# Attention pass, norm, pool table and last pass of a graph network: four programs put into one, by fifths of the nodes

## The chip, the cores and the metric

The kernel runs on one core of one Trainium2 chip. The metric is the device time of one execution in microseconds, less is better; the time of the kernel before is the median of three runs. All data are 32-bit floats except where bf16 is named.

## The reference, cut to what matters

3,125 nodes with 256 features and 53,125 edges (self loops included, sorted by target) go through four layers, each added to x after a layer norm and a rectifier. The change touches what lies between the sums of the third layer and the start of the fourth:

```python
h = jnp.maximum(_layernorm(x, axis=-1), 0.0)
x = x + _L2_gnn_ref(h, src, dst, ...)     # attention, sums over incoming edges
h = jnp.maximum(_layernorm(x, axis=-1), 0.0)
x = x + _L3_gnn_ref(h, edge_weight1, src, dst, ...)
# _L3_gnn_ref:
h = jax.nn.relu(feat @ W_pool.T + b_pool)
m = h[src] * weight
neigh = jax.ops.segment_max(m, dst, num_segments=n)
return feat @ W_self.T + b_self + (neigh @ W_neigh.T + b_neigh)
```

## The kernel before, in words

The nodes are held in SBUF as NB = 25 blocks of NT = 125 rows (`self.x`, `self.h`), and `self.hT` holds h turned around (features on the partitions). The edges are laid out in 128 lanes of LANE = 416 edges each; a pass over the edges walks the 416 steps, and each step gathers one row for each lane by an indirect DMA that GpSimd (POOL) issues.

Every stage is a `nc.Block()` of its own: one instruction stream for each engine, and a barrier of all engines at its end, so no engine begins the next stage before all have finished this one. From the third layer on there are four of them, run in this order by `build`:

1. `attention_pass`: 416 gathers of table rows, logits, exponentials and running sums on VectorE (DVE), states stored by SyncE (SP). Then the lane ends are joined, and 25 gathers (`neigh`, L1811) fetch the final state of each node's last edge, one for each block, five with one semaphore. As a fifth (five blocks) has landed, DVE divides it (L1994, L1996), adds it to x (L2000) and takes the statistics of the five blocks (L550).
2. `normalize("norm3")`: mean and scale of all 25 blocks at once on DVE, square root on ScalarE (ACT), then for each block the normed and rectified h on ACT (L589), two transposes on TensorE (PE, L599) and the copy to `hT` on DVE (L580).
3. `pool_table`: SP loads the three weight matrices and the bias as 125 equal rows, POOL loads the edge weights (L2040, L2043), PE turns the weights, and for each block PE makes two products (L2060), DVE adds the bias into `pool_out` (L2073), ACT rectifies in place (L2079), and SP stores the block to the table in DRAM. SP waits at the end for all stores.
4. `lane_max_pass`: 416 gathers from that table (L2123), each row weighed by ACT (L2148) and taken into a running maximum by DVE (L2234); beside it PE makes the products with W_self, two and a bias product of two rows (L2182, L2184). Then the lane ends are joined, 25 gathers (L2137) bring the maxima, and PE, ACT, DVE and SP finish block by block.

In each engine's stream the order is the order of the code; nothing reorders it. A matmul of 32-bit floats is two instructions in the trace (two passes), a transpose is one.

## Time and profile before

| | |
|---|---|
| median of 3 runs | 2831.26 us (2826.97 to 2834.37) |
| span of the profiled execution, first to last instruction | 2548.0 us |
| own time of the profiled execution | not listed; if it is the median, 283.3 us lie outside the span |
| PE, DVE, ACT, POOL busy in the span | 44%, 56%, 18%, 57% |
| mean granted TensorE clock | 0.698 of 2.4 GHz |

The span is what the trace can explain. The time outside it has no instruction and is taken as it is. Busy shares are averages over stages that have different limits; which engine another one waits for is read from the timeline. Where several instructions stand in one row (x25), its time is the stretch from the first's start to the last's end. PEld is the loading of the stationary matrix.

### The profile page before, as it was taken

What the parts mean: (1) busy time and instruction counts of PE and PEld (TensorE: products, weight loads), DVE (VectorE), ACT (ScalarE), POOL (GpSimd) and SP (SyncE); (2) the same over time, 40 slices, a digit from 0 to 9 for tenths busy, and PEclk for the clock granted to TensorE, in tenths of its full rate; (3) what the DMA queues carried; (4) which work ended last, traced back from release to release, by engine and by line L of the source; (5) the groups of instructions that cost most, each with busy time, mean ns of one, the idle gap of its engine ahead of it and who ended that gap; (6) DMA issues with size and microseconds to landing.
All of it is one profiled execution on the core that took longest, in us unless ns stands there. A gap on an engine that the chain in (4) does not pass through costs nothing. (4 is left out here: it accounts for less than half of the span.)

```text
span 2548.0 us, 19840 instructions
## 1 busy us (share of the span) xinstructions
PE 1127.1 (44%) x4862; PEld 811.0 (32%) x4862; DVE 1431.4 (56%) x3661; ACT 446.7 (18%) x920; POOL 1441.2 (57%) x1472
## 2 busy tenths in 40 slices
PE   5677787777657259999910000000016111111105
PEld 4566776676334135556600000000004000010004
DVE  4377777777999832222246777666754334434432
ACT  3112212221011111111200000000003333333331
POOL 3477777776246030100167777777641777777774
PEclk9799989999766559999955555555557555555557
DMA  4677777775887720000046666666622666666663
GB/s 134 193 233 232 234 232 236 232 232 173 279 266 250 236 61 5 13 10 9 15 125 210 209 208 209 210 210 208 205 66 85 212 210 207 212 212 208 208 212 126
DMA packets 210401, 447.75 MB, mean 176 GB/s; under 512 B 46661, under 2 KB 119226, under 8 KB 210287
## 3 DMA queue, kind: packets, MB, share of 16 engines
q1 hardware_dynamic: 140345, 260.41, 29.0%
q0 software_dynamic: 69136, 185.22, 27.0%
q10 hardware_dynamic: 806, 0.87, 0.1%
q8 instruction: 39, 0.64, 0.1%
q14 instruction: 75, 0.61, 0.1%
HBM read 276.43 MB, written 169.68 MB: 175 GB/s over the span
## 5 line engine op out<-in xcount | busy, mean ns | idle before, releaser
L2123 POOL DMA_INDIRECT best_rows<-message_source_table,lane_source x416 | 393.4, 946 | 166.6 <-issue 126.4
L1797 POOL DMA_INDIRECT att_rows<-att_table,lane_source x416 | 414.5, 996 | 126.7 <-issue 126.7
L711 POOL DMA_INDIRECT msg_rows<-message_source_table,msg_index x416 | 401.5, 965 | 137.9 <-issue 125.3
L2234 DVE SCALAR_TENSOR_TENSOR best_state<-best_state,lane_line,best_ps_rows 128x256 f32<-128x256 f32 x416 | 199.8, 480 | 316.1 <-ACT best_ps_rows L2148 297.8
L841 PE MATMUL msg_ps_sum<-msg_by_edge,msg_rows 128*128 128x128 f32 x1664 | 232.0, 299 | 111.1 <-DVE aggT L771 109.1
L841 PEld LDWEIGHTS msg_ps_sum<-msg_by_edge,msg_rows 128*128 128x128 f32 x1664 | 217.6, 210 | 141.4 <-issue 140.2
L1829 PE MATMUL att_ps_upto<-ident,att_largest 128*4 128x128 f32 x1 | 0.4, 373 | 560.1 <-DVE att_largest L1894 560.1
L2148 ACT ACTIVATE best_ps_rows<-best_rows,lane_weight 128x256 f32<-128x256 f32 x416 | 173.5, 462 | 359.2 <-DMA best_rows<-message_source_table,lane_source 359.2
L2182 PE MATMUL best_ps_self<-w_selfT,hT 128*125 128x256 f32 x100 | 51.7, 672 | 398.5 <-DVE x L2240 387.1
L825 PE MATMUL msg_ps_window<-msg_window,msg_by_node 128*128 128x256 f32 x832 | 210.9, 400 | 17.4 <-DMA msg_window<-message_window_table 14.8
L1453 POOL DMA_INDIRECT att_terms<-aggT,first_edge x25 | 29.5, 1179 | 323.9 <-ACT aggT L1577 323.9
L1916 DVE SCALAR_TENSOR_TENSOR aggT<-aggT,lane_carry,att_rows 128x260 f32<-128x260 f32 x388 | 190.5, 491 | 13.6
L736 DVE TENSOR_TENSOR msg_rows<-msg_ps_window,msg_rows 128x1024 f32<-128x1024 f32 x104 | 127.0, 1221 | 126.0 <-DMA msg_rows<-message_source_table,msg_index 122.8
L796 ACT ACTIVATE msg_rows<-msg_rows 128x1024 f32<-128x1024 f32 x104 | 109.9, 1057 | 435.4 <-DVE msg_rows L736 435.4
L771 DVE TENSOR_TENSOR aggT<-aggT,msg_ps_sum 128x256 f32 x416 | 172.5, 415 | 23.8 <-DVE aggT L771 20.2
L1829 PEld LDWEIGHTS att_ps_upto<-ident,att_largest 128*4 128x4 f32 x1 | 0.1, 83 | 560.9 <-DVE att_largest L1894 560.9
L825 PEld LDWEIGHTS msg_ps_window<-msg_window,msg_by_node 128*128 128x128 f32 x832 | 161.7, 205 | 38.2 <-DVE msg_by_node L724 15.0
L2182 PEld LDWEIGHTS best_ps_self<-w_selfT,hT 128*125 128x125 f32 x100 | 29.0, 320 | 420.8 <-DVE x L2240 403.7
L1909 DVE TENSOR_TENSOR att_rows<-att_rows,att_ps_exps 128x1040 f32<-128x1040 f32 x104 | 127.8, 1229 | 0.0
L1818 ACT ACTIVATE att_ps_exps<-att_logit 128x68 f32<-128x68 f32 (+2 forms) x28 | 6.4, 227 | 547.1 <-DVE att_logit L1901 547.1
L1510 DVE TENSOR_TENSOR x<-x,mlp_ps_o 125x256 f32<-125x256 f32 x25 | 10.5, 421 | 155.9 <-PE mlp_ps_o L1687 155.9
L1674 PE MATMUL mlp_ps_h<-hT,mlp_w 128*128 128x500 f32 (+1 forms) x224 | 95.1, 548 | 0.9 <-ACT mlp_hid L1593 0.9
(317 smaller groups left out, 2161.5 us busy)
## 6 DMA issues: line engine op xcount, KB each, us to landing
att_states<-aggT SPq DMA_DIRECT2D x104, 528.0 KB
msg_window<-message_window_table SPq DMA_DIRECT2D x416, 128.0 KB
best_states<-best_state SPq DMA_DIRECT2D x104, 512.0 KB
attr_states<-attr_work SPq DMA_DIRECT2D x26, 768.0 KB
attr_states<-aggT SPq DMA_DIRECT2D x26, 768.0 KB
attr_work<-in_edge_attr SPq DMA_DIRECT2D x36, 384.0 KB
msg_line<-place_line SPq DMA_DIRECT2D x52, 256.0 KB, 5.0
msg_rows<-message_source_table,msg_index POOLq DMA_INDIRECT x416
```

The source lines that it names most:

```text
L711: nc.gpsimd.indirect_dma_start(rows[:, s, t, :], None, table, bass.IndirectOffsetOnAxis(ap=index[:, s, t:t + 1], axis=0)).then_inc(self.ro ...
L736: nc.vector.tensor_tensor(rows[:, s, :, :], ps_window[s % 2][:], rows[:, s, :, :], ALU.add).then_inc(ev["added"], 1)
L771: nc.vector.tensor_tensor(at, at, ps_sum[s % 2][:, t, :, :], ALU.add).then_inc(tile_added[t], 1)
L796: nc.scalar.activation(rows[:, s, :, :], rows[:, s, :, :], ACT.Relu).then_inc(ev["weighed"], 1)
L825: last = nc.tensor.matmul(ps_window[s % 2][:, t, :], by_node[:, s % BUFS, t * P:(t + 1) * P], window[:, s % BUFS, t, k * window_width:(k + ...
L841: last = nc.tensor.matmul(ps_sum[s % 2][:, t, k, :], rows[:, s, t, k * P:(k + 1) * P], by_edge[:, s % BUFS, t, :], start=True, stop=True)
L1797: nc.gpsimd.indirect_dma_start(rows[:, t % ring, :], None, self.attention_table, bass.IndirectOffsetOnAxis(ap=self.lane_source[:, t:t + 1] ...
L1909: nc.vector.tensor_tensor(of, of, heads(exps(k))[:, :, at:at + TG].rearrange("p h t -> p t h").unsqueeze(3) .to_broadcast([P, TG, H, HS]), ...
L1916: nc.vector.scalar_tensor_tensor(out=state[:, t % held, 0:H * HS], in0=carried[:] if starts else state[:, (t - 1) % held, 0:H * HS], scala ...
L2123: nc.gpsimd.indirect_dma_start(rows[:, g % SLOTS, t, :], None, table, bass.IndirectOffsetOnAxis(ap=self.lane_source[:, g * TG + t:g * TG + ...
L2148: last = nc.scalar.activation(weighed_row(n), rows[:, g % SLOTS, t, :], ACT.Copy, scale=self.lane_weight[:, n:n + 1])
L2234: nc.vector.scalar_tensor_tensor(out=state[:, g % STATE_BUFS, t, :], in0=before, scalar=self.lane_line[:, n:n + 1], in1=weighed_row(n), op ...
```

## The change

Stages 1 to 4 become one Block, `attention_and_best`; the three barriers between them are gone, and semaphores between the engines take their place.

- The weights and their turning, and the loads of the edge weights, move to the head of the attention pass: SP issues three weight loads ahead of its first load, POOL clears `lane_weight` ahead of its first gather and issues the two loads of it before the 416 gathers, PE turns the weights and ACT (not DVE) copies them, ahead of its first exponential.
- The norm goes by fifths: after a fifth is added to x, DVE makes the five blocks' scales (`scales`), ACT the square root, and then ACT makes h of a block, copies the turned block before it to `hT` (`keep`, which DVE did), and rectifies the product of the block before that one (`pool_row`). All five blocks are rectified before ACT takes the next fifth's root.
- The pool product gets a third matmul: `ones[0:1]` by the bias row, which adds the bias in PSUM. DVE's addition of the bias is gone; ACT rectifies out of PSUM into `self.h`, from where SP stores the block.
- POOL waits for all 25 stores before the first gather of the last pass.
- Buffers of the later stages lie in those of the attention pass; PSUM is handed out by whole banks (`late_ps`). The arithmetic and the loops of the two edge passes stay.

```diff
-        k.attention_pass()
-
-        k.normalize("norm3")
-        k.pool_table()
-        k.lane_max_pass("best", k.source_table, k.wT["self"], 3,
-                        {"self": a["L3_gnn_b_self"], "neigh": a["L3_gnn_b_neigh"]})
+        k.attention_and_best()
...
                 @block.gpsimd
                 def _(pool):
+                    nc.gpsimd.memset(lane_weight[:], 0.0).then_inc(weight_cleared, 1)
                     nc.gpsimd.indirect_dma_start(node[:], None, self.attention_table, bass.IndirectOffsetOnAxis(
                         ap=self.lane_node[:, 0:1], axis=0)).then_inc(node_in, 16)
+                    pool.wait_ge(weight_cleared, 1)
+                    for tile, flat in self.by_lanes(lane_weight, a["edge_weight1"].rearrange("e o -> (e o)")):
+                        pool.dma_start(tile, flat).then_inc(listed, 16)
...
+                    pool.wait_ge(stores, 16 * NB)
+                    for g in range(groups):
...
                 @block.scalar
                 def _(act):
+                    for k, name in enumerate(names):
+                        act.wait_ge(w_turned, k + 1)
+                        nc.scalar.copy(wT[name][:], ps_w[k].rearrange("p i o n -> p i (o n)")).then_inc(w_kept, 1)
...
+                    def keep(b):
+                        act.wait_ge(turned, n0 + b + 1)
+                        nc.scalar.copy(self.hT[:, :, b * NT:(b + 1) * NT], ps_turned[b % 2][:, :, 0:NT]
+                                       ).then_inc(kept, 1)
+
+                    def pool_row(b):
+                        act.wait_ge(pooled, b + 1)
+                        nc.scalar.activation(self.h[:, b, :], ps_pool[b % 2], ACT.Relu).then_inc(relued, 1)
+                    for q, blocks in enumerate(parts):
+                        of = slice(blocks.start, blocks.stop)
+                        act.wait_ge(steps_made, c0 + of.stop + 2 * q + 1)
+                        nc.scalar.activation(sd[:, of], sd[:, of], ACT.Sqrt).then_inc(root, 1)
+                        act.wait_ge(rstd, r0 + q + 1)
+                        for b in blocks:
+                            nc.scalar.activation(self.h[:, b, :], self.x[:, b, :], ACT.Relu, scale=rs[:, b:b + 1],
+                                                 bias=nm[:, b:b + 1]).then_inc(made, 1)
+                            if b > blocks.start:
+                                keep(b - 1)
+                            if b > blocks.start + 1:
+                                pool_row(b - 2)
+                        keep(blocks.stop - 1)
+                        for b in range(blocks.stop - 2, blocks.stop):
+                            pool_row(b)
...
+                    def turn(b):
+                        pe.wait_ge(made, n0 + b + 1)
+                        if b >= 2:
+                            pe.wait_ge(kept, n0 + b - 1)
...
+                    def pool_rows(b):
+                        pe.wait_ge(kept, n0 + b + 1)
+                        if b >= 2:
+                            pe.wait_ge(relued, b - 1)
+                        for k in range(2):
+                            nc.tensor.matmul(ps_pool[b % 2], self.hT[:, k, b * NT:(b + 1) * NT], wT["pool"][:, k, :],
+                                             start=k == 0, stop=False)
+                        nc.tensor.matmul(ps_pool[b % 2], self.ones[0:1, 0:NT], pool_bias, start=False, stop=True
+                                         ).then_inc(pooled, 1)
+                    pe.wait_ge(biases_in, 16)
+                    for blocks in parts:
+                        for b in blocks:
+                            turn(b)
+                            if b > blocks.start:
+                                pool_rows(b - 1)
+                        pool_rows(blocks.stop - 1)
...
+                    for q, blocks in enumerate(parts):
+                        attended(q, blocks)
+                        scales(q, blocks)
```

What stands in the streams, at the places that matter. TensorE before, from the end of the attention pass to the first products of the last pass (L599 turns h, L2052 turns weights, L2060 is the pool product, L2182 and L2184 the W_self products; a branch is the end of a stage):

```order
L599 MATMUL norm_ps<-ident,h 128x125 x50
L565 UNCONDITIONAL_BRANCH
L2046 UNCONDITIONAL_BRANCH
L2052 MATMUL pool_ps_t<-ident,pool_raw 128x128 x12
L2060 MATMUL pool_ps<-w_poolT,hT 125x256 x50
L2026 UNCONDITIONAL_BRANCH
L2174 UNCONDITIONAL_BRANCH
L2182 MATMUL best_ps_self<-w_selfT,hT 125x256 x2
L2184 MATMUL best_ps_self<-best_bias,ones 125x256
```

TensorE in the change, the first rows behind the attention pass's lanes (L1933 turns h, L1942 and L1944 are the pool product with its bias product; the turning of the weights, L1904, now stands ahead of the attention pass's own products):

```order
L1933 MATMUL late_ps<-ident,h 128x125 x4
L1942 MATMUL late_ps<-w_poolT,hT 125x256 x2
L1944 MATMUL late_ps<-att_term,ones 125x256
L1933 MATMUL late_ps<-ident,h 128x125 x2
L1942 MATMUL late_ps<-w_poolT,hT 125x256 x2
L1944 MATMUL late_ps<-att_term,ones 125x256
```

The 50 transposes and 50 products that stood in two separate runs now alternate, and behind each pair of products stands the bias product.

ScalarE before, same stretch (L589 makes h, L2079 rectifies, L2148 weighs):

```order
L586 ACT_TABLE_LOAD
L586 ACTIVATE norm_sd<-norm_sd 125x25
L589 ACTIVATE h<-x,norm_nm,norm_rs 125x256 x25
L565 UNCONDITIONAL_BRANCH
L2075 UNCONDITIONAL_BRANCH
L2079 ACTIVATE pool_out<-pool_out 125x256 x25
L2026 UNCONDITIONAL_BRANCH
L2140 UNCONDITIONAL_BRANCH
L2148 ACTIVATE best_ps_rows<-best_rows,lane_weight 128x256 x416
```

ScalarE in the change, from the last h of the first fifth to the first ones of the next (L1872 h, L1860 copy to hT, L1865 rectifying out of PSUM, L1869 root):

```order
L1872 ACTIVATE h<-x,att_term 125x256
L1860 COPY hT<-late_ps 128x2x125
L1865 ACTIVATE h<-late_ps 125x256
L1860 COPY hT<-late_ps 128x2x125
L1865 ACTIVATE h<-late_ps 125x256 x2
L1869 ACTIVATE att_term<-att_term 125x5
L1872 ACTIVATE h<-x,att_term 125x256 x2
```

Behind each h now stand a copy that DVE made before and a rectifier that waits for TensorE, and the next fifth's root stands behind all of the fifth before.

GpSimd before, from the head of the attention pass to the edge weights:

```order
L1789 UNCONDITIONAL_BRANCH
L1791 DMA att_node<-att_table,lane_node 128x268
L1797 DMA att_rows<-att_table,lane_source 128x268 x416
L1804 DMA att_first<-att_states,lane_first 128x264
L1807 DMA att_states<-att_whole,lane_first 53376x264
L1811 DMA aggT<-att_states,last_edge 128x264 x25
L1778 UNCONDITIONAL_BRANCH
L2038 UNCONDITIONAL_BRANCH
L2040 MEMSET lane_weight 128x416
L2043 DMA lane_weight<-in_edge_weight 127x416
```

GpSimd in the change:

```order
L1793 UNCONDITIONAL_BRANCH
L1795 MEMSET lane_weight 128x416
L1796 DMA att_node<-att_table,lane_node 128x268
L1800 DMA lane_weight<-in_edge_weight 127x416
L1800 DMA lane_weight<-in_edge_weight 1x293
L1805 DMA att_rows<-att_table,lane_source 128x268 x416
L1812 DMA att_first<-att_states,lane_first 128x264
L1815 DMA att_states<-att_whole,lane_first 53376x264
L1819 DMA aggT<-att_states,last_edge 128x264 x25
L1826 DMA att_rows<-message_source_table,lane_source 128x256 x416
```

The clearing and the two loads of the edge weights moved ahead of the 416 gathers of the attention pass.

## Rows read from the trace of the kernel before

**Rows 1.** The page: chain that ended last, and the costliest group (part 5).
```profile
POOL 16%; issue 5%; PE 1%; DMA 1%; DVE 0%; POOLq 0%; ACT 0%; DVEq 0%
...
L2123 POOL DMA_INDIRECT best_rows<-message_source_table,lane_source x416 | 393.4, 946 | 166.6 <-issue 126.4
```

**Rows 2.** Timeline, end of attention to start of last pass: start us, us, instruction.
```profile
1870.04 0.28 DVE L1994 RECIPROCAL att_inv<-aggT 125x20 f32<-125x20 f32 x1 [11.47 <-DMA aggT<-att_states,last_edge]
1873.40 1.74 DVE L550 BATCH_NORM_STATS2 stats<-x 125x6 f32<-125x256 f32 x5
1899.18 0.28 DVE L1994 RECIPROCAL att_inv<-aggT 125x20 f32<-125x20 f32 x1 [2.13 <-DMA aggT<-att_states,last_edge]
...
1909.27 12.43 ACT L589 ACTIVATE h<-x,norm_nm,norm_rs 125x256 f32<-125x256 f32 x25 [0.60 <-DVE norm_nm L576]
...
1932.41 22.45 PE L2060 MATMUL pool_ps<-w_poolT,hT 128*125 128x256 f32 x100
...
1955.35 0.42 ACT L2079 ACTIVATE pool_out<-pool_out 125x256 f32<-125x256 f32 x1 [0.45 <-DVE pool_out L2073]
...
1965.03 1.01 POOL L2123 DMA_INDIRECT best_rows<-message_source_table,lane_source  x1 [40.21 <-POOLq L2026]
```

**Rows 3.** Timeline, norm of one block in the MLP stage, all engines.
```profile
1279.90 0.18 DVE L1521 BATCH_NORM_AGGREGATE norm_mv<-stats 125x2 f32<-125x6 f32 x1
...
1280.30 0.20 ACT L1584 ACTIVATE norm_sd<-norm_sd 125x1 f32<-125x1 f32 x1 [5.20 <-DVE norm_sd L1523]
...
1280.93 0.60 ACT L1569 ACTIVATE h<-x,norm_nm,norm_rs 125x256 f32<-125x256 f32 x1 [0.43 <-DVE norm_nm L1527]
1281.59 0.20 PEld L1627 LDWEIGHTS mlp_ps_both<-ident,h 125*128 125x128 f32 x2 [3.12 <-ACT h L1569]
```

**Rows 4.** Timeline, last stage: turning and mixing of a block, PE and ACT.
```profile
2511.48 0.36 PEld L2208 LDWEIGHTS best_ps_rows<-ident,aggT 128*128 128x128 f32 x2
...
2512.11 0.37 ACT L2156 COPY best_neighT<-best_ps_rows 128x256 f32<-128x256 f32 x1 [0.71 <-PE best_ps_rows L2208]
...
2512.56 0.36 PEld L2208 LDWEIGHTS best_ps_rows<-ident,aggT 128*128 128x128 f32 x2
```

**Rows 5.** Timeline, update stage: products of a block with a bias product.
```profile
691.45 1.13 PE L1035 MATMUL upd_ps<-upd_w,hT 128*125 128x256 f32 x4
...
693.37 0.29 PEld L1037 LDWEIGHTS upd_ps<-upd_b_upd,ones 1*125 1x125 f32 x2 [0.33 <-issue]
...
693.99 1.13 PE L1035 MATMUL upd_ps<-upd_w,hT 128*125 128x256 f32 x4
```

**Rows 6.** Groups by line and shape, ACT: count, busy us, mean ns, idle before.
```profile
L1112 ACT ACTIVATE h<-upd_ps 125x256 f32<-125x256 f32 x25 | 9.6, 383 | 145.1 <-PE upd_ps L1037 145.1
...
L374 ACT ACT_TABLE_LOAD x1 | 1.3, 1283 | 3.8 <-issue 3.8
```

**Rows 7.** Windows: busy us of each engine, granted clock (PEclk), DMA share, GB/s.
```profile
core 0: us, PE busy (x) PEld busy (x) DVE busy (x) ACT busy (x) POOL busy (x), PEclk, DMA share, GB/s
1862.00:1909.00 47.00, 0.00 (x0) 0.00 (x0) 27.22 (x67) 1.51 (x2) 27.85 (x25) 0.50 0.27 72
1914.00:1923.00 9.00, 7.24 (x34) 3.29 (x34) 7.42 (x18) 7.69 (x16) 0.09 (x1) 1.00 0.01 2
1966.00:1972.00 6.00, 5.80 (x12) 3.30 (x12) 0.00 (x0) 0.41 (x1) 4.48 (x6) 0.50 0.38 107
2515.00:2548.00 33.00, 24.13 (x122) 19.80 (x120) 8.85 (x21) 7.43 (x20) 11.98 (x13) 0.90 0.45 147
```

**Rows 8.** Timeline, end of the last pass's lanes: last state made, next gather.
```profile
2487.76 2.10 DVE L2234 SCALAR_TENSOR_TENSOR best_state<-best_state,lane_line,best_ps_rows 128x256 f32<-128x256 f32 x4 [2.82 <-ACT best_ps_rows L2148]
...
2493.33 0.94 POOL L2130 DMA_INDIRECT best_first<-best_states,lane_first  x1 [8.48 <-DMA best_states<-best_state]
```

**Rows 9.** Timeline, POOL at the start of the pool-table stage.
```profile
1922.91 0.44 POOL L2040 MEMSET lane_weight<- 128x416 f32 x1 [25.56 <-POOLq L565]
...
1923.66 1.16 POOL L2043 DMA_DIRECT2D lane_weight<-in_edge_weight  x2 [0.30 <-POOL lane_weight L2040]
```

More of the change, by code:

```diff
@@ new lines, in _ @@
+                    act.wait_ge(listed, 32)
+                    for g in range(groups):
+                        act.wait_ge(*later(rows_in[g % SLOTS], 16 * TG * (g // SLOTS + 1)))
+                        for t in range(TG):
+                            n = g * TG + t
+                            if n >= 2 * BUFS and n % 2 == 0:
+                                act.wait_ge(stepped, n + 3 - 2 * BUFS)
+                            last = nc.scalar.activation(weighed_row(n), best_rows[:, g % SLOTS, t, :], ACT.Copy,
+                                                        scale=lane_weight[:, n:n + 1])
+                            if n % 2 == 1:
+                                last.then_inc(weighed, 1)
@@ new lines, in mix @@
+                    def mix(b):
+                        pe.wait_ge(best_kept, b + 1)
+                        if b >= 2:
+                            pe.wait_ge(summed, b - 1)
+                        for k in range(2):
+                            last = nc.tensor.matmul(ps_out[b % 2], neighT[:, b % 2, k, 0:NT],
+                                                    wT["neigh"][:, k, :], start=k == 0, stop=k == 1)
+                        last.then_inc(mixed, 1)
+                    for b in range(NB):
+                        pe.wait_ge(*later(rows_in[b // fifth], 16 * TG * NI + 16 * fifth))
+                        if b >= 2:
+                            pe.wait_ge(best_kept, b - 1)
+                        for k in range(2):
+                            last = nc.tensor.transpose(ps_neigh[b % 2][:, k, :], best_neigh[:, b, k * P:(k + 1) * P],
+                                                       self.ident[:])
+                        last.then_inc(best_turned, 1)
+                        if b > 0:
+                            mix(b - 1)
@@ L1848, in _ @@
+                    mix(NB - 1)
                 @block.vector
@@ L1988, in _, with attended @@
                                             ).then_inc(fixed, 2)
-                    for q in range(5):
-                        some = slice(q * fifth, (q + 1) * fifth)
+                    def attended(q, blocks):
+                        some = slice(blocks.start, blocks.stop)
                         of = neigh[0:NT, some, 0:H * HS].rearrange("p b (h d) -> p b h d", h=H)
```

478 lines of the change are left out of this document (187 added, 291 removed).

## The prediction, made blind

> **What bounds the kernel now.** I read first the chain that ended last. It goes back through the 416 gathers of the last pass and stops at the first of them; what holds it there is GpSimd, which issues one gather every 1.25 us ((393.4 + 126.4) / 416) [rows 1]. So the whole last pass hangs on the moment at which its first gather is issued, 1965.03, and an edit ahead of it is worth what it moves that moment, no more. Then I read the timeline from the landing of the first fifth of attention's sums, 1870.04, to that gather: 94.99 us, in which four things stand in a row [rows 2]. The fifths land 7.29 us apart until 1899.18 ((1899.18 - 1870.04) / 4). ScalarE makes h from 1909.27 on, for 12.43 us. TensorE begins the pool products only at 1932.41 and takes 22.45 us. The last rectifier starts at 1955.35, and the first gather comes 9.68 us after that start, behind the stores and a barrier. Until 1909 TensorE does nothing at all (window 1862:1909) [rows 7]. The reader should see that the stages follow one another although most of the fifths' data are there early, and that what can be won is this overlap.
>
> **What the change adds at the head.** GpSimd clears the edge weights and issues two loads before attention's 416 gathers: from the clearing to the first load 0.75 us, both loads 1.16, a gap of 0.30 [rows 9]: **+2.2 us**, all on the path, since GpSimd's own issue also paces that pass. Bounds: 1 us if they hide in stalls that its first gathers have anyway, 4 us if they are stalled themselves. The three weight loads, twelve transposes and three copies by ScalarE stand there too, but beside some 20 us in which sixteen gathers must be issued before DVE has a batch (16 x 1.25); without that cover they would cost what they cost before, about 9.5 us (1922.91 to 1932.41) [rows 2, 9]. I take 0. One table load more or less: none, in the opening ScalarE takes five roots among rectifiers, by the code, and has a single load of 1.28 us [rows 6]; here it can follow the last exponential at once, long before the first root.
>
> **From the first fifth to ScalarE's first root.** DVE adds and takes statistics until 1873.40 + 1.74 = 1875.14 [rows 2]; the scale chain takes 0.40 us from the first aggregate to the root for one block [rows 3], four more aggregates some 0.07 each: the root at 1875.8, **5.8 us** after the landing.
>
> **A fifth, step by step.** From root to h 0.63, from h to the turn 0.66 [rows 3]; from the turn to ScalarE's copy 0.63, the copy 0.37 [rows 4]: the first pool product starts 2.3 us after the root. Then TensorE's cycle of a block. The update stage has four products and a one-row bias product in 693.99 - 691.45 = 2.54 us [rows 5]. A pair of products alone takes 22.45 / 25 = 0.90 [rows 2], a turn with a pair 2512.56 - 2511.48 = 1.08 [rows 4], so a turn is 0.18, and the new cycle is 2.54 - 0.90 + 0.18 = **1.82 us**. The bias product, 256 columns against one row of weights, costs 2.54 - 1.80 = 0.74, nearly as much as the pair. ScalarE's three pieces of a block, 12.43 / 25 = 0.50, 0.37 and 0.38 [rows 2, 4, 6], are 1.25 us: it is not the bound, TensorE is. But the next root stands behind the last two rectifiers, so the fifths do not overlap: 2.3 + 5 x 1.82 + 0.3 to the last rectifier + 0.3 of it, less the missing turn, is **11.7 us a fifth**. They land every 7.29 us, DVE needs some 6.5 us for one (5.1 to the statistics, 0.7 to the root, 0.6 to h): neither is late again. Five fifths are **58.5 us**.
>
> **The clock.** TensorE comes out of attention at a granted 0.50, the lower level (window 1862:1909) [rows 7]. Its transposes begin 0.66 us after the first h, at 1909.9 [rows 2, 3], and it is at 1.00 by 1914 [rows 7]: some 4 us at half pace, which costs 2 us. At each of four borders it has about 2.5 us with next to nothing to do. The nearest row is the last stage, also fed by fifths: mean 0.90 over 33 us (window 2515:2548) [rows 7], a fifth of the time at the lower level, 3.3 us lost, about 1 for a border. **6 us** in all. Bounds: 0, and 8.5 for each whole fifth at the lower level (below).
>
> **To the first gather.** In the last pass 2493.33 - (2487.76 + 2.10) = 3.47 us lie between a last state made and the gather that waits for its store [rows 8]: **3.5 us**, against 9.68 - 0.42 before.
>
> **Sum.** 5.8 + 58.5 + 6 + 3.5 = 73.8 us where 95.0 stood: -21.2; with +2.2 at the head **-19.0 us**. The span goes from 2548.0 to 2529.0. Both edge passes and the end keep their loops and I cost them at nothing. Nothing in the trace explains the 283.3 us outside the span; I leave them, so the median goes from 2831.3 to **2812.3 us**.
>
> By the Trainium skill, "TensorE: Matmul & The Clock Gate", table "Why this matters for your kernels", a matmul with few rows takes the same time as one with 128. The measured rows disagree: 0.74 us for one row of weights against 0.45, half a pair, for 128 [rows 2, 5]. By the page the third product would take 0.45 and the sum would come to 2805, the first rival.
>
> **Rivals.**
> - The bias product costs no more than half a pair, 0.45. For it: it streams the same 256 columns. Against: in the update stage the loading of its weights comes after 0.33 us of idleness that the profile calls issue, and 0.62 us pass from there to the next product [rows 5]. Then the cycle is 1.53, a fifth 10.2, five 51: -26.5 us, **2805**. The page named above would have it so.
> - The clock stays down for about half of each fifth, because ScalarE's root and h leave TensorE idle five times. At the lower level three products of a block take 3.0 us (twelve passes in 6.0 us, six a block, granted 0.50) (window 1966:1972) [rows 7], the cycle is 3.4, a fifth 20.2: 8.5 more than 11.7. Half of that five times is 21, 15 more than I count: -4 us, **2827**.
> - The other side: the clock never rises. TensorE's load in the last pass shows that a little work every 20 us leaves it at 0.50. 5.8 + 101 + 3.5 + 2.2 = 112.5 against 95.0: +17.5 us, **2849**. It turns to slower once about 25 us are lost, three whole fifths at the lower level. Against it: in 1914:1923 TensorE had only transposes, with gaps, and was granted 1.00.
> - It does not do what it says: the edge pass of attention loses at its head what the tail wins (weight loads of 0.8 MB, ScalarE's copies ahead of its first exponential, a slower first batch), or the time outside the span moves with the merged program: **2831**.
>
> **How the numbers follow.** The forecast, -14 to -24 us for a cycle of 1.8 to 1.95 and 2 to 10 us of clock, has 0.60; the cheap bias product 0.14; the half-cold case 0.12; slower 0.06; no effect 0.08. The range 2800 to 2825 holds the first two and the near part of the third, 0.80. A change of 0.3%, 8.5 us, is about what a measurement of this kernel can tell. Faster by more: 0.60 + 0.14 + two thirds of 0.12 = 0.82; within 0.09; slower 0.09.
>
> **What would show it.** In the changed profile: attention's first gather some 2 us later against the stage's start, and its pace still 1.25 us; the first root 5.8 us after the first fifth; roots 11 to 13 us apart, with the product's cycle at 1.8 to 1.9 and a granted clock of about 0.9; the last rectifier some 64 us after the first root and the first gather 3.5 us behind it. If roots are 7.3 us apart I have TensorE's cycle or the missing overlap wrong; if they are over 15, it is the clock. If all this holds and the time does not move, it is the time outside the span.

## The result, and the profile after

The changed kernel takes 2841.79 us (median of 20 executions, 2829.54 to 2849.05) where the kernel before, run beside it, takes 2828.7 (20 executions, 2816.69 to 2837.74): ratio 1.0052, interval 1.0036 to 1.0068. It is slower by some 13 us, which is the third rival (the clock never rises) and not the forecast.

One thing must be known to read the spans. The execution of the kernel before shown above has a span of 2548.0 us, some 280 us under its timed runs. In another profiled execution of the same kernel (forecast: about 2830 if the short span belonged to the one execution) the span is 2818.9, with 96.1 us from the first landed fifth to the last pass's first gather (95.0 above) and longer edge passes. The short span belonged to that one execution, and spans are compared below with 2818.9 alone. From this second execution, the landed fifth, the first gather, and the chain that ended last (the page, part 4):

```profile
2060.33 0.28 DVE L1994 RECIPROCAL att_inv<-aggT 125x20 f32<-125x20 f32 x1 [11.43 <-DMA aggT<-att_states,last_edge]
...
2156.38 1.01 POOL L2123 DMA_INDIRECT best_rows<-message_source_table,lane_source  x1 [41.35 <-POOLq L2026]
```

```profile
DVE 11%; POOL 4%; issue 4%; another core or an unknown queue 2%; PE 1%; DMA 0%; DVEq 0%; ACT 0%; POOLq 0%; ACTq 0%
```

The first timeline of the kernel after (start us, us, instruction) holds the first landed fifth, its root, the first steps of TensorE, the last bias product with its rectifier, and the first gather of the last pass:

```profile
2071.61 0.28 DVE L2138 RECIPROCAL att_inv<-aggT 125x20 f32<-125x20 f32 x1 [11.50 <-DMA aggT<-att_states,last_edge]
...
2077.29 0.21 ACT L1869 ACTIVATE att_term<-att_term 125x5 f32<-125x5 f32 x1 [17.22 <-DVE att_term L2154]
...
2079.81 1.34 PEld L1942 LDWEIGHTS late_ps<-w_poolT,hT 128*125 128x125 f32 x4 [0.42 <-ACT hT L1860]
...
2082.95 0.29 PEld L1933 LDWEIGHTS late_ps<-ident,h 125*128 125x128 f32 x2 [0.65 <-issue]
...
2086.41 0.29 PEld L1933 LDWEIGHTS late_ps<-ident,h 125*128 125x128 f32 x2 [0.65 <-issue]
```

```profile
2173.31 0.49 PEld L1944 LDWEIGHTS late_ps<-att_term,ones 1*125 1x125 f32 x2 [0.66 <-issue]
...
2174.56 0.38 ACT L1865 ACTIVATE h<-late_ps 125x256 f32<-125x256 f32 x1 [2.76 <-PE late_ps L1944]
...
2177.74 0.95 POOL L1826 DMA_INDIRECT att_rows<-message_source_table,lane_source  x1 [80.95 <-DMA message_source_table<-h]
```

From the landing to the gather it is 2177.74 - 2071.61 = 106.1 us, 11.1 more than in the first execution of the kernel before [rows 2] and 10.1 more than in the second. The first root comes 5.68 us after the landing. Then TensorE takes a block (its turn, its pair of products and the bias product) in 2086.41 - 2082.95 = 3.46 us. Roots stand 19.5 us apart (the second at 2096.86, the fifth at 2155.3). The rectifier of the last block and its store are quick: the gather starts 2.80 us after the rectifier's end.

The products as a group (count, busy us, mean ns), and the same stretch in windows (busy us and count of each engine, granted clock, DMA share, GB/s):

```profile
L1942 PE MATMUL late_ps<-w_poolT,hT 128*125 128x256 f32 x100 | 49.4, 649 | 0.0
L1944 PE MATMUL late_ps<-att_term,ones 1*125 1x256 f32 x50 | 30.3, 707 | 0.0
L1933 PE MATMUL late_ps<-ident,h 125*128 125x125 f32 x50 | 16.0, 441 | 27.2 <-ACT h L1872 27.2
```

```profile
core 0: us, PE busy (x) PEld busy (x) DVE busy (x) ACT busy (x) POOL busy (x), PEclk, DMA share, GB/s
...
2078.00:2098.00 20.00, 17.81 (x40) 9.75 (x40) 6.35 (x18) 6.54 (x17) 14.52 (x15) 0.50 0.47 129
...
2157.00:2176.00 19.00, 19.00 (x44) 10.63 (x42) 0.00 (x0) 5.00 (x14) 0.00 (x0) 0.50 0.11 32
```

The reader is to see two columns together: TensorE has work in 17.5 to 19 of 19 to 20 us, and the granted clock is 0.50, the lower of its levels (1.2 GHz), in all five windows of this length from 2078 to 2176. The pool product took 388 ns a pass in the mean before (L2060, 379 where it ran at the upper level), here 649.

At the head of attention, GpSimd:

```profile
1414.00 0.45 POOL L1795 MEMSET lane_weight<- 128x416 f32 x1 [4.34 <-POOLq L1341]
1414.71 1.17 POOL L1796 DMA_INDIRECT att_node<-att_table,lane_node  x1 [0.27 <-issue]
1415.90 1.15 POOL L1800 DMA_DIRECT2D lane_weight<-in_edge_weight  x2
1417.35 3.40 POOL L1805 DMA_INDIRECT att_rows<-att_table,lane_source  x1 [0.30 <-issue]
```

The clearing takes 1414.71 - 1414.00 = 0.71 us of GpSimd's order and the two loads 1417.35 - 1415.90 = 1.45, together 2.2 us. Whether the attention pass is longer by them can't be seen: from the clearing to the first landed fifth the eleven executions that have this head take 639 to 658 us (657.6 in this one), and the kernel before takes 654.6 in its second execution, from the first gather of the stage.

### The profile page after: what moved, and what is told of

It is laid out like the page before. It is cut to its first block and busy times, and to the rows that moved or that the text cites. A ratio compares the mean times of both kernels' runs of the same rounds, so it can differ in the third digit from the quotient of the medians.

```text
span 2840.9 us, 19920 instructions
## 1 busy us (share of the span) xinstructions
PE 1217.0 (43%) x4912; PEld 858.9 (30%) x4912; DVE 1405.0 (49%) x3619; ACT 462.2 (16%) x952; POOL 1475.4 (52%) x1472
## 5 line engine op out<-in xcount | busy, mean ns | idle before, releaser
L1826 POOL DMA_INDIRECT att_rows<-message_source_table,lane_source x416 | 431.5, 1037 | 207.4 <-issue 125.6
L768 PE MATMUL msg_ps_sum<-msg_by_edge,msg_rows 128*128 128x128 f32 x1664 | 251.1, 310 | 183.9 <-DVE aggT L698 140.8
L768 PEld LDWEIGHTS msg_ps_sum<-msg_by_edge,msg_rows 128*128 128x128 f32 x1664 | 234.4, 221 | 214.9 <-issue 212.9
L1958 PE MATMUL late_ps<-w_selfT,hT 128*125 128x256 f32 x100 | 51.7, 671 | 459.8 <-remote 309.7
L2179 DVE SCALAR_TENSOR_TENSOR att_rows<-att_rows,lane_line,late_ps_share 128x256 f32<-128x256 f32 x208 | 100.0, 481 | 238.8 <-DVE att_rows L2179 89.1
L2179 DVE SCALAR_TENSOR_TENSOR att_rows<-att_rows,lane_line,late_ps 128x256 f32<-128x256 f32 x208 | 99.9, 480 | 165.0 <-DVE att_rows L2179 113.8
L1958 PEld LDWEIGHTS late_ps<-w_selfT,hT 128*125 128x125 f32 x100 | 28.9, 320 | 482.4 <-remote 320.6
L1888 ACT ACTIVATE late_ps_share<-att_rows,lane_weight 128x256 f32<-128x256 f32 x208 | 89.7, 467 | 234.7 <-DVE att_rows L2179 165.3
L2051 DVE TENSOR_TENSOR att_rows<-att_rows,late_ps 128x1040 f32<-128x1040 f32 x104 | 127.8, 1229 | 0.0
L1888 ACT ACTIVATE late_ps<-att_rows,lane_weight 128x256 f32<-128x256 f32 x208 | 89.7, 467 | 176.1 <-DVE att_rows L2179 115.5
```

The lines of the kernel that those rows point to most:

```text
L768: last = nc.tensor.matmul(ps_sum[s % 2][:, t, k, :], rows[:, s, t, k * P:(k + 1) * P], by_edge[:, s % BUFS, t, :], start=True, stop=True)
L1826: nc.gpsimd.indirect_dma_start(best_rows[:, g % SLOTS, t, :], None, self.source_table, bass.IndirectOffsetOnAxis(ap=self.lane_source[:, g ...
L1888: last = nc.scalar.activation(weighed_row(n), best_rows[:, g % SLOTS, t, :], ACT.Copy, scale=lane_weight[:, n:n + 1])
L2051: nc.vector.tensor_tensor(of, of, heads(exps(k))[:, :, at:at + TG].rearrange("p h t -> p t h").unsqueeze(3) .to_broadcast([P, TG, H, HS]), ...
L2179: nc.vector.scalar_tensor_tensor(out=best_state[:, g % STATE_BUFS, t, :], in0=before_it, scalar=self.lane_line[:, n:n + 1], in1=weighed_ro ...
```

## The experiments

All ratios are to the kernel before, run on the same chip beside them. "Stretch" is the time from the first landed fifth to the last pass's first gather, "tail" that from the first landed fifth to the end of the span.

```
kernel                        median us  ratio   interval          stretch   tail
before (once more)            2812.67    0.9986  0.9966 to 1.0005     96.1  758.6
the change                    2841.79    1.0052  1.0036 to 1.0068    106.1  769.3
no bias product               2777.84    0.9853  0.9821 to 0.9885     59.0  720.1
bias product, 128 rows        2786.56    0.9895  0.9868 to 0.9921     65.4  727.3
bias product, 64 rows         2824.02    1.0046  1.0029 to 1.0063     99.3  762.1
warmed, 28 products           2827.89    1.0043  1.0023 to 1.0063    107.4  768.5
warmed, 44 products           2833.83    1.0075  1.0051 to 1.0099    116.4  779.1
borders closed                2816.46    1.0025  1.0007 to 1.0043     97.4  760.4
128 rows, borders closed      2780.01    0.9874  0.9850 to 0.9898     62.5  724.5
the same, again               2795.74    0.9902  0.9881 to 0.9922     54.6  717.1
bias added by VectorE         2832.73    1.0028  1.0012 to 1.0044     97.3  758.8
128 rows, then one            2818.27    0.9977  0.9959 to 0.9995     87.1  749.1
```

Tail less stretch is 661 to 663.2 us in every one of them; the first fifth lands anywhere from 2050 to 2072. So behind the landing the stretch carries the whole effect, and what is left over in a ratio is the part ahead, which moves by far more than the head of the change can explain. A stretch is that of the one profiled execution of its row, a median that of all timed ones. Three profiled executions were the fastest of theirs by 5 to 13 us: with 64 rows (2814.35), with the bias added by VectorE (2817.96) and the second with both repairs (2776.27).

### The third product taken out

```diff
-  nc.tensor.matmul(ps_pool[b % 2], hT[:, k, block], wT["pool"][:, k, :], start=k == 0, stop=False)
-  nc.tensor.matmul(ps_pool[b % 2], self.ones[0:1, 0:NT], pool_bias, start=False, stop=True)
+  nc.tensor.matmul(ps_pool[b % 2], hT[:, k, block], wT["pool"][:, k, :], start=k == 0, stop=k == 1)
```

(hT[:, k, block] is short for self.hT[:, k, b * NT:(b + 1) * NT]. This kernel leaves the bias out of its result and only serves to find the cause.)

> The changed kernel without the third product: the pool table is made without its bias, so the output lacks b_pool; everything else stays. Theory A (the one-row product in every block keeps TensorE at the lower level of its clock, 0.50 in the changed kernel's whole table stage): the clock goes to 1.00 in the first fifth, a block takes about 1.1 us, roots lie 8 to 9 us apart instead of 19.5, the stretch from the first landed fifth to the first gather of the last pass falls from 106 us to 55 to 60; about 48 us less than the changed kernel, ratio to the kernel before 0.985 to 0.99. Theory B (the emptying of the pipeline at each fifth keeps the clock down, the product is only its own time): the clock stays at 0.50, a block takes about 2.2 us, roots lie 13 to 14 us apart, the stretch is about 80 us, ratio to before 0.995.

```profile
2056.00:2070.00 14.00, 0.00 (x0) 0.00 (x0) 5.86 (x16) 0.62 (x2) 10.85 (x11) 0.50 0.36 97
...
2080.00:2090.00 10.00, 7.75 (x30) 5.44 (x29) 4.70 (x14) 5.13 (x15) 7.62 (x7) 0.83 0.57 169
...
2100.00:2110.00 10.00, 8.05 (x31) 5.76 (x32) 6.04 (x19) 6.36 (x18) 0.00 (x0) 0.83 0.22 68
```

And two stretches of the second fifth, TensorE alone (busy us and count, granted clock, DMA share, GB/s):

```profile
2082.00:2084.00 2.00, 2.00 (x7) 0.50 0.48 144
2086.00:2088.00 2.00, 1.81 (x8) 1.00 0.52 157
```

2777.84 us, ratio 0.9853. The clock rises within the first fifth. The 0.79 to 0.83 of the long windows is a mean of the two levels: behind a border, where TensorE has stood still, the clock is 0.50, and later in the same fifth it is 1.00 again. So borders do take the clock down here, without a one-row product, but it comes back. Fifths are 9.9 us apart in the mean. Everything else of the change stands as it was, so the loss sits in the third product.

### The same product with 128 rows

The added rows are ones in row 0 of the weights and zeros below it, so the sum is the same; VectorE fills both tiles ahead of time.

```diff
-  nc.tensor.matmul(ps_pool[b % 2], self.ones[0:1, 0:NT], pool_bias, start=False, stop=True)
+  nc.tensor.matmul(ps_pool[b % 2], first_row, bias_rows, start=False, stop=True)   # [128, NT], [128, D]
```

> The changed kernel with a bias product of 128 rows: the stationary tile has ones in row 0 and zeros in 127 rows, the moving tile has the bias in row 0 and zeros below, so the same sum and the same 256 columns, but no change of the number of rows between products. Theory A: the clock rises to 1.00 in the first fifth, a block takes about 1.55 us without gaps, roots 10 to 11 us apart, stretch 62 to 68 us, ratio to before 0.987 to 0.991. Theory B: the clock stays at 0.50, a block takes 3.1 us, roots 18 us apart, stretch about 100 us, ratio to before 1.002.

```profile
2068.00:2079.00 11.00, 10.45 (x40) 8.02 (x40) 5.51 (x14) 5.23 (x14) 8.56 (x9) 0.74 0.43 117
2079.00:2089.00 10.00, 5.36 (x25) 3.85 (x26) 5.77 (x16) 3.93 (x10) 6.92 (x7) 1.00 0.50 148
...
2099.00:2109.00 10.00, 8.32 (x42) 6.55 (x41) 5.87 (x19) 6.06 (x18) 0.00 (x0) 1.00 0.22 67
```

2786.56 us, ratio 0.9895. The count of products is that of the change and their columns too; only the rows in use differ, and the clock is at 1.00 from the second fifth on. A block takes 1.51 us (turns at 2074.25 and 2075.76). The product costs 6.3 us of stretch against none at all (65.4 and 59.0), where one row costs 47. Most of the 6.3 lies in the first two fifths (13.5 and 12.8 us), where ScalarE's rectifiers start up to 3.2 us after the recorded end of their products (the product of 2085.25 ends at 2085.84, its rectifier starts at 2089.05); the third and fourth take 9.9 each, against 9.3 and 9.6 without the product.

### Between the two: 64 rows

```diff
-  nc.tensor.matmul(ps_pool[b % 2], first_row, bias_rows, start=False, stop=True)
+  nc.tensor.matmul(ps_pool[b % 2], first_row[0:64, :], bias_rows[0:64, :], start=False, stop=True)
```

> As the run with the bias product of 128 rows, but the product takes 64 rows (ones in row 0, zeros in the other 63). Theory A1 (what costs is how few rows the third product uses; it grows gradually as they get fewer): something between, a pooling product of at most 0.5 us behind the two others, granted clock between 0.50 and 1.00, stretch from the first landed fifth to the first last-pass gather 66 to 85 us, ratio to before 0.990 to 0.998. Theory A2 (any product of fewer rows than the array's 128 breaks the run of products, and the clock stays at its lower level with it): as the changed kernel, block cycle 3.4 us, clock 0.50, stretch 106 us, ratio 1.005. Theory A3 (only a product of very few rows does it): as with 128 rows, cycle 1.51 us, stretch 65 us, ratio 0.9895.

```profile
core 0: us, PE busy (x), PEclk, DMA share, GB/s
2058.00:2080.00 22.00, 20.34 (x47) 0.50 0.42 117
2080.00:2090.00 10.00, 8.37 (x35) 0.98 0.19 57
2090.00:2144.00 54.00, 50.69 (x116) 0.51 0.11 33
```

In these windows, of TensorE alone, the columns are busy us and count, granted clock, DMA share and GB/s. Nearly as with one row: ratio 1.0046, stretch 99.3. The clock was up in one fifth of the five (it took 12.9 us, the others 19.3 to 19.6) and fell again with the same products. Rise and fall both come in the first block behind a border. The profiled execution was also the fastest of seven (2814.35, median 2824.02), so the others may well lack that fifth. So it is no matter of very few rows alone (A3 falls, and A1's range too). A2 is nearest, but too wide in its words: the turns have 125 rows (ident,h 125*128) and the run with 128 rows in the bias product holds 1.00 with them. Where the change to fewer rows begins to cost lies between 64 and 125 rows, and no run narrows it. This run also shows that it isn't the new tiles or their place that help, since it uses the same ones.

### Is it the drain at the borders?

The rival to the product itself was that TensorE stops at each border of the fifths. Here the next root and first h go ahead of the last two rectifiers:

```diff
-                            if b > blocks.start:
+                            if b > 0:
                                 keep(b - 1)
-                            if b > blocks.start + 1:
+                            if b > 1:
                                 pool_row(b - 2)
-                        keep(blocks.stop - 1)
-                        for b in range(blocks.stop - 2, blocks.stop):
-                            pool_row(b)
...
-                    for blocks in parts:
-                        for b in blocks:
-                            turn(b)
-                            if b > blocks.start:
-                                pool_rows(b - 1)
-                        pool_rows(blocks.stop - 1)
+                    for b in range(NB):
+                        turn(b)
+                        if b > 0:
+                            pool_rows(b - 1)
+                    pool_rows(NB - 1)
```

(ScalarE's last copy and last two rectifiers now stand once, behind all blocks.)

> The changed kernel, one-row product kept, but the borders of the fifths are closed up: the next fifth's root and first rectified block go ahead of the last two rectifiers of the one before, and TensorE's order runs on over the borders. If the clock stays down because TensorE drains at the five borders (theory B), it rises to 1.00 within a fifth or two: cycle 1.8 us, stretch under 75 us, ratio under 0.994. If it is the one-row product (theory A), the clock stays 0.50 and only the borders are saved: 19.5 - 5 x 3.46 = 2.2 us at each of four, 9 us: stretch 97 us, ratio 1.002.

```profile
2064.00:2144.00 80.00, 80.00 (x186) 0.50 0.20 58
```

This is the plainest line of the study: 80.00 of 80 us busy, no gap in TensorE's records (whose ends are modelled), and a granted clock of 0.50. The borders are worth 8.7 us (106.1 to 97.4; 9 expected), the clock didn't move, and the rival falls: without borders the clock doesn't rise either.

### Can the one-row product hold a clock that is up?

Two tries put full products ahead of the first fifth:

```diff
+                    pe.wait_ge(shares, 2)
+                    for _ in range(28):      # 44 in the second
+                        nc.tensor.matmul(ps_pool[1], wT["self"][:, 0, 0:NT], wT["self"][:, 1, :], start=True, stop=True)
                     pe.wait_ge(biases_in, 16)
```

> The changed kernel with 28 products of 128 rows and 256 columns put on TensorE while it waits for the first fifth; they write to a bank that the first pool product overwrites. They take about 18 us at mixed clock and so end near the first turn. Theory A in its strict form (with the one-row product in every block the clock can't be held): 1.00 at the first turn, 0.50 within the first fifth or two, roots 17 to 19.5 us apart after it, stretch 100 us or more. The other form (once up it stays up, only the rise fails): roots about 12 us apart, stretch about 70 us, ratio to before 0.992. Theory B: falls back at the first border between fifths, stretch 98 to 102 us.

> The changed kernel with 44 added full products ahead of the first fifth in place of 28; the 28 ended 5.7 us before the first turn, and the clock had fallen by then. 44 take 14.17 us x 44/28 = 22 us at most and so last until the first turn or some us beyond it. If the fifths' own work can hold the upper level but not reach it (theory H), the clock stays 1.00 in the first fifth and at least until its end: block cycle about 1.8 us there. If the one-row product keeps the clock down whatever it was before (theory A), it falls to 0.50 inside the first fifth, and the block cycle is 3.4 us again in the later part of it and in the four others; stretch 95 to 106 us, ratio 1.002 to 1.005.

```profile
2046.00:2051.00 5.00, 5.00 (x25) 4.36 (x24) 0.00 (x0) 0.00 (x0) 3.78 (x5) 1.00 0.32 85
...
2056.00:2060.00 4.00, 0.00 (x0) 0.00 (x0) 3.29 (x14) 0.51 (x2) 3.10 (x3) 0.75 0.37 98
...
2064.00:2084.00 20.00, 17.07 (x40) 9.31 (x39) 5.96 (x17) 6.09 (x16) 11.21 (x12) 0.50 0.42 119
```

```profile
2046.00:2063.00 17.00, 17.00 (x82) 1.00 0.35 94
...
2066.00:2070.00 4.00, 0.00 (x0) 0.52 0.40 108
```

Neither answers. The 28 products ended 5.7 us ahead of the first turn, and the clock had fallen. The 44 reached it, but ScalarE's first copy came at 2069.58, 6.5 us after the recorded end of the transposes that it waits for, and the clock fell in that gap. They did show that full products alone bring the clock up here. With 44 the first fifth took 29.9 us, and so the stretch is the longest of all, 116.4, outside the 95 to 106 expected.

The third try changes the product midway: 128 rows in the first ten blocks, one row in the other fifteen. The edit is shown against the kernel with 128 rows:

```diff
+                        rows = P if b < 10 else 1
-                        nc.tensor.matmul(ps_pool[b % 2], first_row, bias_rows, start=False, stop=True
+                        nc.tensor.matmul(ps_pool[b % 2], first_row[0:rows, :], bias_rows[0:rows, :], start=False, stop=True
```

> The bias product has 128 rows in the first two fifths (blocks 0 to 9) and one row in the other three. With 128 rows the clock was 1.00 from the middle of the first fifth on. Theory A (the one-row product pulls the clock down whatever it was before): clock 0.71 in the first fifth, 1.00 in the second, and back to 0.50 within the third; the last two fifths 19.5 us each; stretch 5.7 + 13.5 + 12.8 + about 15 + 19.5 + 19.5 + 3.5 = 85 to 90 us; ratio 0.997 to 1.000. Theory H (it can't raise the clock but holds it): 1.00 to the end, fifths of 11.7 us, stretch 5.7 + 13.5 + 12.8 + 3 x 11.7 + 3.5 = 70.6 us, ratio 0.991 to 0.993.

TensorE, from the third fifth (one row) into the fourth, and its windows:

```profile
2104.40 0.69 PE L1948 MATMUL late_ps<-att_term 1*125 1x256 f32 x2
...
2106.25 0.69 PE L1948 MATMUL late_ps<-att_term 1*125 1x256 f32 x2
...
2113.95 0.93 PE L1936 MATMUL late_ps<-ident,h 125*128 125x125 f32 x4 [1.63 <-ACT h L1875]
...
2115.91 1.21 PE L1948 MATMUL late_ps<-att_term 1*125 1x256 f32 x2
...
2119.37 1.21 PE L1948 MATMUL late_ps<-att_term 1*125 1x256 f32 x2
```

```profile
2105.00:2115.00 10.00, 8.31 (x36) 1.00 0.22 66
2115.00:2125.00 10.00, 10.00 (x26) 0.54 0.08 26
```

Both theories had a part of it. In the third fifth the one-row product runs at the upper level: a block in 2106.25 - 2104.40 = 1.85 us, the fifth in 2112.65 - 2101.14 = 11.5. Then the clock falls in the first block of the fourth, whose bias product already takes 1.21 us in place of 0.69, and it doesn't rise again: the fourth fifth takes 18.3 us and every later window says 0.50. Stretch 87.1 us (85 to 90 by theory A), ratio 0.9977; that the stretch fits is in part luck, since the first two fifths took 16.0 and 13.2 us (late rectifiers again) and the third 11.5 in place of about 15. The fall came some 2 us behind a border in which TensorE had stood still for 1.63 us; the kernel with 128 rows throughout has such borders too, and keeps 1.00. Read together with the run without the product, where the clock falls behind a border and comes back, the one-row product seems less to push the clock down than to keep it from coming up. This is a reading; one fifth of the 64-row run goes against it, and no run has the fifths with a raised clock, one-row products and no border.

### Both repairs together

The bias product with 128 rows and the closed borders (the two edits above), timed twice:

> The bias product of 128 rows and the closed borders together. Cycle 1.51 us as with 128 rows alone: 25 x 1.51 = 38 us, with 5.8 us ahead of the first root, 2.5 us to the first product, 3.5 us behind the last and about 1 us per border: 52 to 56 us against 65.4 us with 128 rows alone, 95.0 us before. Ratio to the kernel before 1 - (95.0 - 54 - 1.7)/2820 = 0.986 (0.985 to 0.9895). If instead the borders were hidden already (the fifths wait on VectorE's roots, not on the drain), it is 65 us and ratio 0.9895.

> The kernel with the bias product of 128 rows and closed borders once more, with its own runs of the kernel before. In its first profile the blocks 8 to 10 took 5 us each in place of 1.51, ScalarE's rectifier starting 1.6 us after the recorded end of the products, with the clock falling to 0.50 behind it; about 3 x 3.5 = 10 us were lost so. If that belonged to the one execution, the stretch is now 52 to 56 us where it was 62.5, and the ratio 0.984 to 0.988. If it comes with the program, the same stall shows again near the same blocks, stretch 60 to 65 us, ratio 0.987 to 0.989.

The first: the bias products of the fifth and the sixth block on TensorE (2074.04 and 2077.05), and ScalarE's copy and its rectifiers of these two blocks:

```profile
2074.04 0.59 PE L1947 MATMUL late_ps<-att_term 128*125 128x256 f32 x2
...
2075.66 0.37 ACT L1863 COPY hT<-late_ps 128x250 f32<-128x250 f32 x1 [0.64 <-PE late_ps L1936]
...
2077.05 0.59 PE L1947 MATMUL late_ps<-att_term 128*125 128x256 f32 x2
...
2079.23 0.38 ACT L1868 ACTIVATE h<-late_ps 125x256 f32<-125x256 f32 x1 [3.20 <-issue]
...
2084.27 0.38 ACT L1868 ACTIVATE h<-late_ps 125x256 f32<-125x256 f32 x1 [3.16 <-PE late_ps L1947]
```

The second, in two windows:

```profile
2065.00:2075.00 10.00, 9.70 (x40) 0.83 0.41 122
2075.00:2110.00 35.00, 33.87 (x168) 1.00 0.37 111
```

The second has the stretch that was forecast, 54.6 us, with fifths of 8.0 to 9.0 us; the first has 62.5, and the difference is in the blocks shown: by ScalarE's order the rectifier at 2079.23 waits for the products that by the record ended at 2074.63, and the one at 2084.27 for those that ended at 2077.64. They come 4.6 and 6.6 us late, with nothing in the trace that holds them. (The expectation for the second execution counted these blocks as 8 to 10 and set the first rectifier against the wrong products.) The second execution has no such delay above 1.7 us, so it isn't in every execution; but that one was the fastest of its seven (2776.27, median 2795.74), and how many of the timed ones have the delay isn't known. Ratios are 0.9874 and 0.9902, on either side of the 0.9895 of 128 rows alone: the 10.8 us of stretch that the closed borders take off in the trace are not told apart from nothing by these timings. Both beat the kernel before.

### The bias by VectorE, in fifths

```diff
+                    def add_bias(b):
+                        dve.wait_ge(pooled, b + 1)
+                        nc.vector.tensor_tensor(self.h[:, b, :], ps_pool[b % 2], pool_bias, ALU.add).then_inc(biased, 1)
...
                     for q, blocks in enumerate(parts):
                         attended(q, blocks)
                         scales(q, blocks)
+                        for b in blocks:
+                            add_bias(b)
```

(Cut: VectorE's wait for the bias, the product's end without a third matmul, and ScalarE's rectifier, which now works in place.)

> The changed kernel without the third product: VectorE adds the pool bias out of PSUM, as the kernel before did, ScalarE rectifies in place; the fifths stay, and VectorE's additions of a fifth stand in its order behind the next attention scale of its own fifth. Theory A (the one-row product keeps the clock down, and the fifths by themselves pay): clock 0.8 to 0.85 as without the product, fifth of 10 to 12 us, stretch 60 to 66 us, ratio 0.986 to 0.990. Rival (VectorE becomes the bound: five additions per fifth wait behind the next fifth's 6.5 us of scale, sum and statistics, TensorE stops for two blocks, and the clock stays at 0.50): fifth of 17 to 20 us, stretch 92 to 105 us, ratio 0.999 to 1.005.

VectorE, from the last addition of the second fifth to the third's scale:

```profile
2100.29 0.42 DVE L2164 TENSOR_TENSOR h<-late_ps,att_term 125x256 f32<-125x256 f32 x1 [0.44 <-PE late_ps L1943]
2100.63 0.27 DVE L2137 RECIPROCAL att_inv<-aggT 125x20 f32<-125x20 f32 x1
...
2106.10 0.17 DVE L2153 TENSOR_SCALAR att_term<-att_term 125x5 f32<-125x5 f32 x1
```

The rival's mechanism is there: the attention scale of the next fifth waits behind five additions and then takes 5.5 us in which TensorE has nothing. Its numbers are met only in sum: 97.3 us and ratio 1.0028. The fifths stand 15.8 to 16.5 us apart, under its 17 to 20, at clocks of 0.5 to 0.84, and the first takes 27.6: in it VectorE's third, fourth and fifth additions start 2.9, 8.4 and 6.7 us after the recorded end of their products (the fourth pair ends at 2071.91, its addition starts at 2080.29). With a first fifth like the others the stretch would be about 86 us, an estimate from these lengths. So taking the third product away isn't enough by itself, it matters what takes its place. An order in which VectorE takes the next fifth's scale ahead of the additions was not run.

## Why the prediction was wrong

- **What bounds the kernel**: that the gather's start carries the whole tail was right (tail less stretch the same within 2.5 us in all twelve executions of the table). That GpSimd's issue paces the last pass was read from the one short execution, whose chain has POOL 16% and DVE 0% [rows 1]; in the second it is DVE 11% and POOL 4% (shown above), and the last maximum ends 34 us behind the last gather's start. This changes no term of the sum.
- **The head**, +2.2 us: the rows after give 2.2 in GpSimd's order. That all of it is on the path isn't shown: in the second execution of the kernel before, GpSimd waits 59 us for VectorE in attention's gathers, so its issue doesn't pace that pass throughout either.
- **Landing to root**, 5.8 us: 5.68. **Root to first product**, 2.3: 2079.81 - 2077.29 = 2.5.
- **The block's cycle at the upper level**, 1.82 us, and **the fifth**, 11.7: 1.85 and 11.5, in the only fifth where a one-row product ran at that level. These terms of the sum were right.
- **The clock is the step that failed.** The prediction took 6 us for it, from the last stage's mean of 0.90 [rows 7]. That stage is fed by fifths, but holds no product on one row in each block. In the change every block ran at the lower level: 3.46 us a block, 19.5 a fifth, 39 us more over five than 5 x 11.7, of which the sum held 6. The 33 us that it lacked are the difference between the forecast stretch of 73.8 and the measured 106.1, to within 1 us. The case itself stood among the rivals, with a chance of 0.06. The argument against the rival, that transposes alone were granted 1.00 in 1914:1923 [rows 7], was true and about another mixture of work. The row that stood nearest was the update stage's bias product [rows 5], whose granted clock I had not read. Windows of the kernel before show both levels in that stage, with one one-row product to four full ones:

```profile
670.00:690.00 20.00, 16.81 (x37) 0.55 0.57 186
690.00:700.00 10.00, 9.10 (x35) 1.00 0.93 284
```

  The cycle of 2.54 us came from the second of them. With one to two, as in the change, no window of the fifths came up.
- **The other side's price**, +17.5 us: it had 3.4 us a block and 20.2 a fifth; it was 3.46 and 19.5. The last store to the gather took 2.80 in place of 3.5. So 106.1 + 2.2 = 108.3 against the rival's 112.5. That is some 12 us over the 96.1 of the second execution before; 13.1 were measured, with the head's 2.2 not shown by itself.
- **The cheap bias product** (rival 1) is false for one row and true for 128: 1.51 us a block against the rival's 1.53. The Trainium skill, "TensorE: Matmul & The Clock Gate", table "Why this matters for your kernels", says that a matmul with few rows takes as long as one with 128. Between products of 128 rows it does not hold here: at the upper level a block takes 1.85 us with one row and 1.51 with 128.
- **The time outside the span**, 283.3 us, was no property of the kernel: in every other profiled execution here it is 2 us. It did not enter the sum.

What is shown: the one-row product in each block is the cause of the loss. Without it, or with zeros up to 128 rows, the same order of work is granted the upper level and the kernel is faster than the one before (0.9853, without the bias in its result, and 0.9895); with zeros up to 64 rows, in the same tiles, it is not (1.0046). Closing the borders or two tries to warm the engine ahead did not help.

What stays open is why the chip grants less with it. One difference stands in the traces: before the weights of a one-row or 64-row product, and again before the next turn, the loading of weights stands still for 0.65 us at the lower level (the two [0.65 <-issue] and the [0.66 <-issue] shown above) and for 0.33 at the upper, and then starts together with its matmul. With 128 rows it starts 0.1 to 0.2 us ahead of its matmul and the loads follow one another within 0.1 us, the turns of 125 rows too (from the run with 128 rows, whose matmul of this bias product starts at 2083.74):

```profile
2083.53 0.40 PEld L1947 LDWEIGHTS late_ps<-att_term 128*125 128x125 f32 x2
...
2083.96 0.36 PEld L1936 LDWEIGHTS late_ps<-ident,h 125*128 125x128 f32 x2
```

So the array may stand still twice in each block although TensorE's records, with their modelled ends, leave no gap: 80.00 of 80 us busy doesn't rule this out. Whether this, or the share of rows in use, sets the grant, no run separates. Open too are the late starts behind TensorE's work.

## What to carry to other kernels

A bias added on TensorE by a product of one row is not a small extra: check the granted clock in a stretch that holds such a product before giving it a price, and if the engine sits at its lower level while it is busy, pad the product with zeros to all 128 rows (64 did not do here). Price a stage at both levels when it is TensorE that bounds it; a rival that hangs on the clock needs a row with the same mixture of work, not the nearest one in time. And compare the stretch that the change touches, from one event to another in each trace, since the median of the whole moves by more than the effect: the kernel before had medians from 2812.4 to 2828.7 us in these sets of runs. Profile the kernel before twice where its span and its timed runs differ: the short execution here had another chain.

## What the runs showed of the hardware

- Busy and clock are two things: 80.00 us of 80 busy at a granted 0.50, with one-row products among full ones; 33.87 of 35 at 1.00 with 128-row ones.
- More rows, all zeros, made a product cheaper: the stretch is 34 us shorter with 128 rows than with 64, the ratio 0.9895 in place of 1.0046. At the same upper level a block takes 1.51 us with 128 rows and 1.85 with one or with 64.
- A clock once up was kept through 11.5 us of blocks with the one-row product (2104.40 to 2115.91), fell in the first block behind a border, and did not rise again in the two fifths left.
- Work that waits for TensorE started late by its recorded end in several executions: 6.5 us with 44 warming products, 4.6 and 6.6 in the first with both repairs, 8.4 and 6.7 with the bias by VectorE (there it is VectorE that starts late), up to 3.2 with 128 rows, 3.1 in the run with 128 rows and then one. Each time TensorE had been at 1.00 and the node gathers were still being issued or had ended less than 4 us before. No run isolates it, and since the ends are modelled, the work itself may have ended late.
